# Summing a scan's output states: GpSimd adds halves of every other unit in the first chunk

## The chip, the cores and the metric

The kernel runs on one core of a Trainium2 chip. The metric is the device time of one execution in microseconds (us). TensorE is PE in the profile, VectorE is DVE, ScalarE is ACT, GpSimd is POOL, SyncE (which issues the DMAs here) is SP.

## The reference

The input is 64 series of 750 samples. Each is cut into 10 patches of 128 samples, hop 64, so there are 640 tokens. What is computed for them, all in float32:

```python
h = patches @ tok_W.T + tok_b                        # 512 wide
h = h + attn(layernorm(h))                           # attn: see below
h = h + swiglu(layernorm(h))                         # 512 -> 2048 -> 512
# attn(x): x + mamba(rmsnorm(x)), then + swiglu(rmsnorm(.))
# mamba(x):
z, xv, Bm, Cm, dt_in = split(x @ in_proj_w.T)
dt = softplus(dt_in @ dt_proj_w.T + dt_proj_b)       # 1024 channels
h[t] = exp(dt[t] * A) * h[t-1] + dt[t] * x[t] * B[t] # 16 states per channel
y[t] = sum over the 16 states of C[t] * h[t]
out = ((y + D_skip * x) * silu(z)) @ out_proj_w.T
```

The sum over 16 states in the line for y is what the change is about.

## The kernel before

The layout is features on the 128 partitions, tokens along the free axis. The tokens are worked in two chunks: c = 0 with 290 tokens (29 series of 10) and c = 1 with 350.

The recurrence is cut into **units**. The 1024 channels are KI = 8 tiles (m) of 128 channels; the 16 states of a channel are QU = 4 quarters (q) of NQ = 4 states. Unit u of a chunk is the pair (m, q), so there are 32 units in each chunk, 64 in all. For each unit:

- SP loads `bb` (rows of B spread over the partitions, line 359) and `cb` (rows of C, line 375) from DRAM, 580 KB each in chunk 0. `load_b(u)` is issued in the slot of unit u - 2. The rows of C of a tile m were stored before by `store_c` (line 363) from `c_rows`, which ScalarE copies from a PSUM bank at line 629.
- GpSimd makes the input term, `hs` = dtx * bb (`input_term`, line 443), for the four states at once, 128 x 1160 elements in chunk 0; at q = 0 it first makes `dtx` (line 433). `hs` has NH = 4 buffers.
- ScalarE makes the decay, exp(dt * A), in PSUM (`da`, line 538).
- VectorE scans (line 734), one state at a time, and multiplies by C, two states at a time (`times_c`, line 745), writing into `hs` again.
- The four states are summed. In chunk 0 TensorE does it (`state_sum`, line 949): four products with the identity matrix, accumulated over the tile's four units in the PSUM bank `work[SUM]`. Every float32 product shows as two records in the trace, so a unit has eight. In chunk 1 GpSimd adds (`add_states`, lines 456 to 469) into `acc`, and TensorE sums only two halves per tile (`ysum`).
- VectorE's `gate_y` (lines 758, 762) takes the finished sum of a tile, in the slot of the next tile's unit q = 1.

All engines go through the same list of **slots**, `schedule()`, one for each unit, with other work (**steps**) put into each: the projections `in_dt`, `in_x`, `in_b`, `in_c`, `in_z`, `dtp`, `xs` for later tiles, then for chunk 1 (`tokc`, `mean`, `ln1`, `rms1`), and in the slots of chunk 1 the MLP of chunk 0. The order on every engine is fixed by this list. ScalarE and VectorE take some steps one slot later than TensorE (`late(slots, 1)`), GpSimd and SP two slots later.

- TensorE, slot of unit u: part of the steps, then `state_sum(u - 2)`, then the other steps; when u % 4 is 1 the sum comes first. `xs`, `dtp`, `in_c` and `in_z` use a ring of three PSUM banks, so one waits until ScalarE has read the step three before it.
- GpSimd, slot of unit u: `input_term(u + 1)`, then `add_states(u - 1)` (which did nothing in chunk 0), then the steps: `softplus` (lines 475, 477, 479, the last one writes `dt`), which stands in the even slots that have a `dtp`. `input_term(u)` waits for its `bb` and for the state sum of unit u - 4, whose buffer it takes.
- ScalarE: decays for the next unit, and between them the steps. Its own part of the softplus (lines 655 to 662) waits for GpSimd's softplus of the tile before (`dt_ready`).

Of the kernel before, what the change touches and what calls it, by code (L numbers as in the profile page):

```python
# [29 lines left out]
KI = DI // P  # L30
HT = HID // P
NQ = 4
QU = NS // NQ
# [36 lines left out]
def unit_of(u):  # L70

    return u // UNITS, u % UNITS // QU, u % QU


def piece(u, p):
    c = u // UNITS
    return PIECE0[c] + u % UNITS * NP[c] + p


def products_through(u):  # L80

    return piece(u, NP[u // UNITS] - 1) // 2 + 1
# [60 lines left out]
def late(slots, lag, kinds=LATE):  # L143
    def lag_of(i, s):
        return lag if i == 1 or (s[0] in kinds and slots[i][0] is not None) else 0
    return [(unit, [s for j in range(max(0, i - lag), i + 1) for s in slots[j][1] if lag_of(j, s) == i - j])
            for i, (unit, _) in enumerate(slots)]
# [30 lines left out]
def build(nc, patches, tok_w, small, w_in, w_dt, w_stream, out):  # L178
# [10 lines left out]
    with ExitStack() as ctx:  # L189
# [3 lines left out]
        def sem(name):  # L193
            return ctx.enter_context(nc.semaphore(name))
# [70 lines left out]
        scan_done, c_times, th_done = sem("scan_done"), sem("c_times"), sem("th_done")  # L265
        added, h_summed, skip_done, y_done = sem("added"), sem("h_summed"), sem("skip_done"), sem("y_done")
# [12 lines left out]
        def full(eng, name):  # L279
            b, n = uses[last_name(name)]  # L280
            eng.wait_ge(bank_full[b], n + 1)
# [4 lines left out]
        def freed(eng, name):  # L286

            b, n = uses[name]
            eng.wait_ge(bank_free[b], n + 1)
# [4 lines left out]
        def h(c, k):  # L294
            return h_all[:, k, OFF[c]:OFF[c] + TS[c]]

        def a(c, k):
            return a_all[:, k, OFF[c]:OFF[c] + TS[c]]
# [20 lines left out]
        def on_dve(k):  # L319
            return k % DVE_SHARE == DVE_SHARE - 1  # L320
# [5 lines left out]
        def splits_at(s):  # L326
            if s == ("out", NCH - 1, KD - 2):
                return range(NW - 1)
            if is_split(s) and split_of[s] + NW - 1 < SPLITS:
                return [split_of[s] + NW - 1]  # L330
            return []

        def adds_through(u):

            return 7 * (u // QU - KI) + 2 * (u % QU) + 1

        block = ctx.enter_context(nc.Block())

# [79 lines left out]
        @block.gpsimd  # L418
        def _(pool):
            def split_low(k):  # L420
                pool.wait_ge(w_hi_done, k + 1)
                nc.gpsimd.tensor_tensor(ws[:, k % NW, 1, :], wraw[:, split_loads[k] % NRAW, :],  # L422
                                        ws[:, k % NW, 0, :].bitcast(F32), ALU.subtract).then_inc(w_lo_pool, 1)

            def input_term(u):
                c, m, q = unit_of(u)
                t, n = c * KI + m, TS[c]
                if q == 0:
                    pool.wait_ge(dt_ready, t + 1)
                    freed(pool, ("xs", c, m))  # L430
                    if t >= 2:
                        pool.wait_ge(dbx_done, QU * (t - 1))
                    nc.gpsimd.tensor_tensor(dtx[:, t % 2, 0:n], dt[:, m, 0:n], xf[:, m, 0:n],
                                            ALU.mult).then_inc(dtx_done, 1)
                    pool.wait_ge(dtx_done, t + 1)
                pool.wait_ge(bb_loaded[u % NB], 16 * (u // NB + 1))
                if u >= NH:
                    v = u - NH
                    if v < UNITS:
                        pool.wait_ge(h_summed, v + 1)  # L440
                    else:
                        pool.wait_ge(added, adds_through(v + 1 if v % QU == 0 else v))
                nc.gpsimd.tensor_tensor(hs[:, u % NH, 0:NQ * n].rearrange("p (n t) -> p n t", t=n),  # L443
                                        dtx[:, t % 2, 0:n].unsqueeze(1).to_broadcast([P, NQ, n]),
                                        bb[:, u % NB, 0:NQ * n].rearrange("p (n t) -> p n t", t=n),
                                        ALU.mult).then_inc(dbx_done, 1)

            def add_states(u):
                c, m, q = unit_of(u)
                if c == 0:  # L450
                    return
                w = 2 * TS[c]
                lo, hi = hs[:, u % NH, 0:w], hs[:, u % NH, w:2 * w]
                pool.wait_ge(c_times, products_through(u))
                if q <= 1:
                    nc.gpsimd.tensor_tensor(lo, lo, hi, ALU.add).then_inc(added, 1)
                if q == 0:
                    return
                n, total = adds_through(u), acc[:, 0:w]
                if q == 1:  # L460
                    if m >= 1:
                        full(pool, ("ysum", c, m - 1))
                    pool.wait_ge(added, n - 1)
                    nc.gpsimd.tensor_tensor(total, hs[:, (u - 1) % NH, 0:w], lo, ALU.add).then_inc(added, 1)
                else:
                    pool.wait_ge(added, n - 2)
                    nc.gpsimd.tensor_tensor(total, total, lo, ALU.add).then_inc(added, 1)  # L467
                    pool.wait_ge(added, n - 1)
                    nc.gpsimd.tensor_tensor(total, total, hi, ALU.add).then_inc(added, 1)

            def softplus(c, m):
                i, n = KI * c + m, TS[c]
                pool.wait_ge(sp_act, 3 * i + 3)

                nc.gpsimd.tensor_tensor(sp_u[:, 0:n], sp_w[:, 0:n], sp_u[:, 0:n], ALU.subtract).then_inc(sp_small, 1)
                pool.wait_ge(sp_small, 2 * i + 1)
                nc.gpsimd.tensor_tensor(sp_l[:, 0:n], sp_l[:, 0:n], sp_u[:, 0:n], ALU.subtract).then_inc(sp_small, 1)
                pool.wait_ge(sp_small, 2 * i + 2)
                nc.gpsimd.tensor_tensor(dt[:, m, 0:n], dt[:, m, 0:n], sp_l[:, 0:n], ALU.add).then_inc(dt_ready, 1)

            def residual(c, o):
                pool.wait_ge(res_done, KD * c + o + 1)
                nc.gpsimd.tensor_tensor(h(c, o), h(c, o), a(c, o), ALU.add).then_inc(hres_done, 1)

            for i, (unit, steps) in enumerate(late(slots, 2)):
                if unit == 0:
                    input_term(0)
                if unit is not None and unit + 1 < NCH * UNITS:
                    input_term(unit + 1)
                if unit is not None and unit >= 1:  # L490
                    add_states(unit - 1)
                if i == len(slots) - 1:
                    add_states(NCH * UNITS - 1)
                for s in steps:
                    if s[0] == "dtp":
                        softplus(s[1], s[2])
                    for k in splits_at(s):
                        if not on_dve(k):
                            split_low(k)
                    if s[0] == "out":  # L500
                        residual(s[1], s[2])

        @block.scalar
        def _(act):
# [51 lines left out]
            def gated_high(n):  # L556
                act.wait_ge(gated_raw, n + 1)
                gated_free(act, n)
                if n == 4 * HH * (NCH - 1):
                    act.wait_ge(added, adds_through(NCH * UNITS - 1))  # L560
                nc.scalar.copy(gated[:, 0, n % HH, 0:TS[NCH - 1]], gated_f[:, n % 2, 0:TS[NCH - 1]]).then_inc(gated_hi, 1)
# [364 lines left out]
        def _(pe):  # L926
# [15 lines left out]
            def state_sum(u):  # L942
                c, m, q = unit_of(u)
                n = TS[c]
                if q == 0 and m >= 1:
                    pe.wait_ge(y_done, m)
                pe.wait_ge(c_times, products_through(u))
                for i in range(NQ):
                    last = nc.tensor.matmul(work[SUM][:, 0:n], sm[:, S_IDENT:S_IDENT + P], hs[:, u % NH, i * n:(i + 1) * n],  # L949
                                            start=(q == 0 and i == 0), stop=(q == QU - 1 and i == NQ - 1))  # L950
                last.then_inc(h_summed, 1)

            def split_products(w, x, *ready):
# [169 lines left out]
```

## Time and profile before

| what | value |
|---|---|
| median of 3 runs | 705.84 us (lowest 703.69) |
| profiled execution | 703.4 us |
| its span, first to last instruction | 701.6 us |
| PE busy | 645.4 us, 92% |
| DVE busy | 427.3 us, 61% |
| POOL busy | 422.7 us, 60% |
| ACT busy | 340.9 us, 49% |
| chain that ended last | PE 62%, DVE 14%, DMA 10%, issue 5%, ACT 4%, POOL 4% |
| units of chunk 0 | about 34 to 213 us of the span |

Busy time is the union of an engine's instructions. The chain that ended last is followed back from the last instruction, at each step to what released it. PE records are pipelined, so the duration of a group in a timeline is from its first start to its last end. Times in timelines and windows count from the start of the span.

### The profile page before, as it was taken

What the parts mean: (1) busy time and instruction counts of PE and PEld (TensorE: products, weight loads), DVE (VectorE), ACT (ScalarE), POOL (GpSimd) and SP (SyncE); (2) the same over time, 40 slices, a digit from 0 to 9 for tenths busy, and PEclk for the clock granted to TensorE, in tenths of its full rate; (3) what the DMA queues carried; (4) which work ended last, traced back from release to release, by engine and by line L of the source; (5) the groups of instructions that cost most, each with busy time, mean ns of one, the idle gap of its engine ahead of it and who ended that gap; (6) DMA issues with size and microseconds to landing.
All of it is one profiled execution on the core that took longest, in us unless ns stands there. A gap on an engine that the chain in (4) does not pass through costs nothing.

```text
span 701.6 us, 8678 instructions
## 1 busy us (share of the span) xinstructions
PE 645.4 (92%) x2878; PEld 513.4 (73%) x2878; DVE 427.3 (61%) x660; ACT 340.9 (49%) x649; POOL 422.7 (60%) x236
## 2 busy tenths in 40 slices
PE   5969897799986989999979999999999999899998
PEld 3647674466554657777756777765799999799998
DVE  5097787898885878877986988871323132332132
ACT  4368889358886843323333323311444353543441
POOL 0276667445774999977784788743454655255551
PEclk9979999999999899999998999999999999999999
DMA  8788987499799797988784988842443444243521
GB/s 346 237 294 288 333 265 292 153 332 309 240 402 375 240 385 255 346 294 327 280 316 141 344 325 307 286 126 84 132 139 122 149 137 135 61 136 117 165 68 42
DMA packets 49164, 163.50 MB, mean 233 GB/s; under 512 B 4320, under 2 KB 18528, under 8 KB 48480
## 3 DMA queue, kind: packets, MB, share of 16 engines
q1 hardware_dynamic: 49120, 162.95, 66.7%
q8 instruction: 23, 0.38, 0.2%
q14 instruction: 21, 0.17, 0.1%
HBM read 145.24 MB, written 17.69 MB: 232 GB/s over the span
## 4 chain that ended last, share of the span: by engine, by line
PE 62%; DVE 14%; DMA 10%; issue 5%; ACT 4%; POOL 4%; SPq 0%; DVEq 0%; ACTq 0%; POOLq 0%
PE work L939 48%; PE da L939 13%; DMA bb<-b_rows 8%; DVE da L734 8%; DVE hs L745 3%; POOL hs L443 3%; ACT da L538 1%; PE work L949 1%; DMA b_rows<-sq 1%; DMA c_rows<-c_rows 1%; DMA sm<-small 0%; DVE work L758 0%; DVE a L796 0%; DVE gated_n L852 0%; DVE sq L813 0%
## 5 line engine op out<-in xcount | busy, mean ns | idle before, releaser
L734 DVE TENSOR_TENSOR_SCAN da<-da,hs 128x290 f32<-128x290 f32 (+1 forms) x256 | 198.3, 817 | 58.7 <-POOL hs L443 44.9
L443 POOL TENSOR_TENSOR hs<-dtx,bb 128x1160 f32<-128x1160 f32 (+1 forms) x64 | 171.0, 2676 | 79.0 <-DMA bb<-b_rows 40.1
L538 ACT ACTIVATE da<-dt,a_neg 128x261 f32<-128x261 f32 (+1 forms) x256 | 118.1, 494 | 134.1 <-DVE hs L745 133.9
L422 POOL TENSOR_TENSOR ws<-wraw,ws 128x1024 fp32r<-128x1024 f32 x40 | 101.4, 2536 | 92.8 <-ACT ws L546 92.8
L939 PE MATMUL work<-sq,wraw 128*128 128x290 f32 x512 | 126.5, 407 | 3.7 <-DVE sq L813 2.1
L939 PEld LDWEIGHTS work<-sq,wraw 128*128 128x128 f32 x512 | 96.4, 189 | 33.7 <-issue 5.1
L939 PE MATMUL work<-hn,win 128*128 128x290 f32 (+1 forms) x336 | 104.9, 462 | 16.1 <-DVE hn L804 8.0
L745 DVE TENSOR_TENSOR hs<-da,cb 128x580 f32<-128x580 f32 (+1 forms) x128 | 105.2, 822 | 7.1 <-DVE sq L829 0.2
L939 PEld LDWEIGHTS work<-hn,win 128*128 128x128 f32 x336 | 66.6, 202 | 50.5 <-issue 21.8
L546 ACT CAST ws<-wraw 128x1024 fp32r<-128x1024 f32 x48 | 50.3, 1048 | 70.9 <-PE work L939 36.0
L939 PE MATMUL work<-hn,ws 128*128 128x350 f32 x456 | 75.3, 323 | 1.6 <-DVE hn L900 1.6
L939 PEld LDWEIGHTS work<-hn,ws 128*128 128x128 f32 x456 | 73.4, 189 | 1.9 <-issue 1.9
L949 PE MATMUL work<-hs,sm 128*128 128x290 f32 x256 | 70.0, 417 | 0.0
L939 PE MATMUL work<-gated_n,wraw 128*128 128x290 f32 x256 | 64.1, 408 | 1.1 <-DVE gated_n L852 1.1
L949 PEld LDWEIGHTS work<-hs,sm 128*128 128x128 f32 x256 | 49.8, 195 | 17.6 <-issue 1.0
L939 PEld LDWEIGHTS work<-gated_n,wraw 128*128 128x128 f32 x256 | 48.3, 189 | 16.2 <-DVE gated_n L852 2.1
L939 PE MATMUL da<-hn,ws 128*128 128x350 f32 x312 | 51.7, 323 | 0.0
L939 PEld LDWEIGHTS da<-hn,ws 128*128 128x128 f32 x312 | 50.3, 189 | 0.0
L467 POOL TENSOR_TENSOR acc<-acc,hs 128x700 f32<-128x700 f32 x16 | 26.7, 1668 | 33.5 <-DVE hs L745 33.5
L846 DVE TENSOR_TENSOR pair<-th,work 128x350 f32<-128x350 f32 x20 | 10.4, 520 | 56.5 <-PE work L939 53.4
L939 PE MATMUL work<-gated,ws 128*128 128x350 f32 x240 | 39.3, 323 | 0.0
L939 PEld LDWEIGHTS work<-gated,ws 128*128 128x128 f32 x240 | 38.8, 188 | 0.0
(107 smaller groups left out, 669.1 us busy)
## 6 DMA issues: line engine op xcount, KB each, us to landing
wraw<-w_stream SPq DMA_DIRECT2D x104, 512.0 KB, 4.0
bb<-b_rows SPq DMA_DIRECT2D x32, 700.0 KB, 6.7
cb<-c_rows SPq DMA_DIRECT2D x32, 700.0 KB, 4.8
bb<-b_rows SPq DMA_DIRECT2D x32, 580.0 KB, 8.6
cb<-c_rows SPq DMA_DIRECT2D x32, 580.0 KB, 7.5
c_rows<-c_rows SPq DMA_DIRECT2D x8, 875.0 KB, 9.1
c_rows<-c_rows SPq DMA_DIRECT2D x8, 725.0 KB, 5.4
win<-w_in SPq DMA_DIRECT2D x4, 1024.0 KB, 13.0
```

What stands on the lines that cost most here:

```text
L422: nc.gpsimd.tensor_tensor(ws[:, k % NW, 1, :], wraw[:, split_loads[k] % NRAW, :], ws[:, k % NW, 0, :].bitcast(F32), ALU.subtract).then_inc ...
L443: nc.gpsimd.tensor_tensor(hs[:, u % NH, 0:NQ * n].rearrange("p (n t) -> p n t", t=n), dtx[:, t % 2, 0:n].unsqueeze(1).to_broadcast([P, NQ, ...
L467: nc.gpsimd.tensor_tensor(total, total, lo, ALU.add).then_inc(added, 1)
L538: last = nc.scalar.activation(dst, src, ACT.Exp, scale=a_neg[:, j:j + 1])
L546: nc.scalar.copy(ws[:, k % NW, 0, :], wraw[:, i % NRAW, :]).then_inc(w_hi_done, 1)
L734: nc.vector.tensor_tensor_scan(da[:, k % ND, 0:w], da[:, k % ND, 0:w], hs[:, u % NH, p * w:(p + 1) * w], 0.0, ALU.mult, ALU.add).then_inc( ...
L745: nc.vector.tensor_tensor(hs[:, u % NH, here].rearrange("p (i w) -> p i w", w=w), da[:, k % ND:k % ND + 2, 0:w], cb[:, u % NC, here].rearr ...
L846: nc.vector.tensor_tensor(gated_f[:, i % 2, 0:n], th[:, i % 2, 0:n], bank((s, "up")), ALU.mult).then_inc(gated_raw, 1)
L939: last = nc.tensor.matmul(dst, w, x, start=(k == 0), stop=(k == len(pairs) - 1))
L949: last = nc.tensor.matmul(work[SUM][:, 0:n], sm[:, S_IDENT:S_IDENT + P], hs[:, u % NH, i * n:(i + 1) * n], start=(q == 0 and i == 0), stop ...
```

## The change

In chunk 0, for units with odd q, `add_states` on GpSimd now waits for the unit's products and adds the second half of `hs` (states 3 and 4 of the unit, 580 columns) onto the first, in place. TensorE's `state_sum` for these units waits for that add instead of for the products, and sums two blocks of 290 columns instead of four. Units with even q are as they were. `adds_through`, which counts GpSimd's adds for the semaphore `added`, gets the 16 new adds.

```diff
         def adds_through(u):
 
-            return 7 * (u // QU - KI) + 2 * (u % QU) + 1
+            c, m, q = unit_of(u)
+            return 2 * (u // QU) + (q + 1) // 2 if c == 0 else 2 * KI + 7 * (u // QU - KI) + 2 * q + 1
...
             def add_states(u):
                 c, m, q = unit_of(u)
-                if c == 0:
+                if c == 0 and q % 2 == 0:
                     return
                 w = 2 * TS[c]
                 lo, hi = hs[:, u % NH, 0:w], hs[:, u % NH, w:2 * w]
                 pool.wait_ge(c_times, products_through(u))
-                if q <= 1:
+                if c == 0 or q <= 1:
                     nc.gpsimd.tensor_tensor(lo, lo, hi, ALU.add).then_inc(added, 1)
-                if q == 0:
+                if c == 0 or q == 0:
                     return
...
-                pe.wait_ge(c_times, products_through(u))
-                for i in range(NQ):
+
+                k = NQ - 2 * (q % 2)
+                if q % 2 == 1:
+                    pe.wait_ge(added, adds_through(u))
+                else:
+                    pe.wait_ge(c_times, products_through(u))
+                for i in range(k):
                     last = nc.tensor.matmul(work[SUM][:, 0:n], sm[:, S_IDENT:S_IDENT + P], hs[:, u % NH, i * n:(i + 1) * n],
-                                            start=(q == 0 and i == 0), stop=(q == QU - 1 and i == NQ - 1))
+                                            start=(q == 0 and i == 0), stop=(q == QU - 1 and i == k - 1))
                 last.then_inc(h_summed, 1)
```

## Rows read from the trace of the kernel before

**Rows 1.** The page, busy time, share of the span and instructions of each engine.

```profile
PE 645.4 (92%) x2878; PEld 513.4 (73%) x2878; DVE 427.3 (61%) x660; ACT 340.9 (49%) x649; POOL 422.7 (60%) x236
```

**Rows 2.** Who waited for whom, 34 to 232 us: total, times, longest.

```profile
DVE da L734 <- POOL hs L443: 44.1, 13, 18.9
POOL hs L443 <- DMA bb<-b_rows: 36.8, 14, 5.7
```

**Rows 3.** The chain that ended last, one cycle: start us, us, what.

```profile
81.59 2.45 POOL hs L443
...
92.72 0.34 ACT c_rows L629
...
93.49 9.89 DMA bb<-b_rows
```

**Rows 4.** GpSimd's timeline: start us, us, instruction, idle time before and its releaser.

```profile
83.99 0.80 POOL L475 TENSOR_TENSOR pair<-sp_w,pair 128x290 f32<-128x290 f32 x1
...
86.30 4.84 POOL L443 TENSOR_TENSOR hs<-dtx,bb 128x1160 f32<-128x1160 f32 x2
...
97.42 2.45 POOL L443 TENSOR_TENSOR hs<-dtx,bb 128x1160 f32<-128x1160 f32 x1 [3.11 <-issue]
...
144.51 2.43 POOL L443 TENSOR_TENSOR hs<-dtx,bb 128x1160 f32<-128x1160 f32 x1 [10.42 <-PE work L949]
```

**Rows 5.** ScalarE's timeline, softplus steps and one copy of c_rows.

```profile
64.43 0.51 ACT L655 ACTIVATE pair<-work,sm 128x290 f32<-128x290 f32 x1 [1.61 <-POOL dt L479]
...
86.39 0.49 ACT L655 ACTIVATE pair<-work,sm 128x290 f32<-128x290 f32 x1
...
89.70 0.39 ACT L629 COPY c_rows<-work 128x290 f32<-128x290 f32 x1
...
178.39 0.55 ACT L655 ACTIVATE pair<-work,sm 128x350 f32<-128x350 f32 x1 [0.71 <-issue]
...
228.98 0.55 ACT L655 ACTIVATE pair<-work,sm 128x350 f32<-128x350 f32 x1 [0.60 <-issue]
```

**Rows 6.** Windows: length, busy time of each engine, granted clock, DMA share, GB/s.

```profile
59.60:81.50 21.90, 21.41 (x85) 15.34 (x85) 17.03 (x25) 17.24 (x37) 14.85 (x11) 1.00 0.86 286
...
88.75:90.20 1.45, 0.86 (x4) 0.34 (x2) 1.36 (x4) 1.45 (x5) 1.45 (x1) 1.00 0.00 0
...
180.20:182.50 2.30, 1.86 (x7) 0.88 (x5) 1.39 (x4) 2.27 (x7) 2.30 (x2) 1.00 0.00 0
183.40:231.00 47.60, 40.26 (x134) 25.46 (x133) 34.54 (x48) 37.02 (x70) 29.17 (x21) 0.94 1.00 362
```

**Rows 7.** GpSimd's groups by shape: count, busy us, mean ns, idle before.

```profile
L443 POOL TENSOR_TENSOR hs<-dtx,bb 128x1160 f32<-128x1160 f32 x32 | 77.9, 2442 | 64.3 <-DMA bb<-b_rows 32.8 <-PE work L949 20.6 <-issue 10.7
...
L467 POOL TENSOR_TENSOR acc<-acc,hs 128x700 f32<-128x700 f32 x16 | 26.7, 1668 | 33.5 <-DVE hs L745 33.5
...
L433 POOL TENSOR_TENSOR dtx<-dt,xf 128x290 f32<-128x290 f32 x8 | 6.4, 800 | 0.7 <-ACT xf L639 0.7
```

**Rows 8.** TensorE's timeline around the sums of units 7 and 31.

```profile
81.96 2.12 PE L949 MATMUL work<-hs,sm 128*128 128x290 f32 x8
...
87.41 2.19 PE L939 MATMUL work<-hn,win 128*128 128x290 f32 x8 [2.30 <-ACT dt L656]
...
226.24 1.50 PE L939 MATMUL work<-sq,sm 32*128 32x350 f32 x2 [4.98 <-ACT z L645]
227.67 4.24 PE L949 MATMUL work<-hs,sm 128*128 128x290 f32 x8
```

**Rows 9.** The chain again: the sum of unit 13, and 263 us.

```profile
120.69 1.96 PE work L949 x8
...
263.12 63.19 PE work L939 x256
```

**Rows 10.** VectorE's timeline, a scan of unit 36.

```profile
246.22 1.67 DVE L734 TENSOR_TENSOR_SCAN da<-da,hs 128x350 f32<-128x350 f32 x2 [0.82 <-POOL hs L443]
```

**Rows 11.** Windows, a stretch at the half clock.

```profile
225.60:232.30 6.70, 6.06 (x12) 3.71 (x13) 5.31 (x7) 5.99 (x13) 6.54 (x6) 0.50 0.62 256
```

## The prediction

> **What bounds the kernel now.** I began with the page's sums: TensorE is busy 92% of the span and GpSimd 60%, which would make any work taken off TensorE look welcome [rows 1]. But shares are means over stages, so I next read who waits for whom between 34 and 232 us, the stretch in which the change lives. There the long waits are not TensorE's: VectorE's scans wait 44 us for GpSimd's input terms, and these wait 37 us for the loads of `bb` [rows 2]. The chain in order of time shows a loop. The `bb` of unit 9 has landed, GpSimd multiplies at 81.59, VectorE scans, ScalarE copies `c_rows` at 92.72, SP then issues the next `bb`, and that takes 9.89 us to land at 103.4 [rows 3]. That is 21.9 us for four units, most of it DMA. The windows tell where this loop has air: between 88.75 and 90.20, and again between 180.20 and 182.50, the DMA engines move nothing, though they are busy before and after; from 183.40 to 231.00 they are busy all the time [rows 6]. So in the steady part the DMA engines work off a queue, run dry, and wait until ScalarE's copy of `c_rows` (89.70) lets SP store it and issue the next loads [rows 5]. What makes ScalarE late makes the next four units late.
>
> What makes it late? ScalarE's timeline says it: its softplus step at line 655 waits for GpSimd's `dt` at 64.43 (1.61 us idle, released by POOL dt L479) and again at 178.39 after 0.71 us. At 86.39 it shows no wait, but there GpSimd's last softplus instruction ended at 86.30, where its next product starts [rows 4, 5]. So the chain of waits names VectorE and the DMA, and GpSimd's softplus ends at the same moment: a hidden twin of the path with about 0.1 us of slack. TensorE in the same cycle has `in_c` done long before it is copied, and idles before 87.41 for ScalarE [rows 8].
>
> **The change, part by part.** *TensorE* loses two of four products in 16 of 32 units. One unit's eight records take 1.96 us on the chain at the full clock [rows 9], so 0.98 us goes each time, 15.7 us in all. Most of that is not on the path: TensorE waits for ScalarE in every cycle [rows 8]. It counts in one place, 116 to 125 us, where the chain runs through TensorE (first steps of the second chunk) and holds the sums of units 12 and 13; unit 13's halves: -0.98 us [rows 9].
>
> *GpSimd* gains 16 adds with an output of 128x580. No such form is in the trace. Bounds: 700 elements take 1.67 us, 290 take 0.80 us, 1160 (a product that also reads two inputs) take 2.44 us [rows 7]. By proportion, 580 elements give 1.38 us; the line through 290 and 700 gives 0.80 + 290 x 2.12 ns = 1.41 us, the one through 290 and 1160 gives 0.80 + 290 x 1.89 ns = 1.35 us. I take 1.38, since the same adds of the second chunk are its nearest kin; 16 x 1.38 = 22 us of GpSimd work.
>
> Against the slower engine the Trainium skill (GPSIMD Engine Reference, Engine selection) says that an elementwise add belongs on VectorE, GpSimd being about twice as slow with two inputs. No row shows VectorE adding this form; it would not alter the sum, which uses GpSimd's own rows.
>
> *Where the adds stand.* GpSimd adds unit u right behind the input term of u + 2 and ahead of the softplus of that slot. Behind it are queued that softplus, then the input term of u + 3; ScalarE's softplus waits for the first and VectorE's scan for the second. Its wait for the products is free in the steady part: VectorE is done with unit 7 and waits for unit 9's input term [rows 2], and the add of unit 7 would start at 84.0, when that term ends. GpSimd was idle before that term, but the add stands behind it, so the idle time can't be used. There are six kinds of places:
> - Units 3, 7, 11 and 23 (softplus taken by ScalarE at 64.43, at 86.39, a cycle later, and at 178.39 [rows 5]): the full 1.38 us goes into ScalarE, then into the `c_rows` copy or the `z` behind it, and the DMA engines (or TensorE, after unit 11) stay idle that much longer. 4 x 1.38 = +5.5 us. Two of the four are seen in the waits, one is argued from the 0.1 us of slack, one is its repetition a cycle later.
> - Units 1, 5, 9, 13, 25, 29: GpSimd idles after the softplus (3.11 us before 97.42 [rows 4]); the adds are hidden there. With that cover gone they would cost 1.38 each, 8 us.
> - Units 15, 17, 19: no softplus in these slots, and VectorE is the busy engine; unit 17's add makes GpSimd wait for VectorE, but GpSimd had 10.42 us of idle time there, until TensorE's sum let it go on at 144.51 [rows 4]. 0.
> - Unit 21: its softplus delays ScalarE by 1.3 us, ScalarE has about that much air before unit 25. +0.1.
> - Unit 27: delays ScalarE too, but the DMA queue is never empty from 183.40 to 231.00, as the weight preload stands in it [rows 6]; loads issued later land when the queue allows. 0; if the queue were not full, +1.4.
> - Unit 31: on TensorE eight records take 4.24 us at the half clock [rows 8, 11], four would take 2.1. But its add pushes the softplus, for which ScalarE waits at 228.98 [rows 5], and with it the bank that TensorE's next product needs. VectorE's scan at 246.22 waits for GpSimd too, which sets the pace there [rows 10]. Between -0.9 and +1.4; I take +0.5.
>
> *TensorE's new wait.* The sum of unit 7 began at 81.96; now it begins at about 85.4, when the add is done, and ends at 86.5. Behind it are queued `xs` and the next `in_c`, and this waited for ScalarE until 87.41 anyway [rows 8]. VectorE's gate reads the sum behind unit 9's scans, later still. So the wait is under cover by 0.9 us, and by 2.3 with ScalarE late as well.
>
> **Sum.** +5.5 - 1.0 + 0.1 + 0.5 = +5.1 us. From 263 us on the chain is mostly TensorE products that the change doesn't touch, 63 us of them in one piece at the start [rows 9], so a shift at its start is a shift of the end. Against the profiled execution (703.4 us, span 701.6) that gives 708.5; against the median of 705.84, 710.9. The shown runs are 703.69 and 705.84, so I take the middle, 709.7.
>
> **Rivals.**
> 1. *The clock.* Waits lengthen TensorE's idle stretches: before the sum of unit 7 by some 3.4 us. In the trace an idle stretch of 4.98 us before 226.24 went with the half clock from 225.60 to 232.30 (1.2 instead of 2.4 GHz), one of 2.3 us before 87.41 did not [rows 8, 11]. At the half clock a full state sum costs 4.24 instead of 2.12 us. If every late add brought on a stretch of 6.7 us, and the products in it lay on the path, each of the four cycles would lose up to 3.4 us more: 13.6 + 5.1 = +18.7, 724 us, slower by over 2%. It decides only when `in_c` and what follows end after ScalarE's turn to copy them, some 3 us later than now (87.41 + 2.19 against 92.72) [rows 3, 8]; the half clock adds about 2 us to one projection. So it should stay mostly covered, except near 120 us, where it could cost 1 to 3 us. The Trainium skill (TensorE: Matmul & The Clock Gate, Why this matters for your kernels) warns of idle gaps between bursts for this reason; the trace agrees at 226 us.
> 2. *TensorE is the bound after all.* If TensorE's queue held back ScalarE in each cycle, the 15.7 us would come back: up to 690 us. Against it: TensorE waits for ScalarE's banks in every cycle, and the DMA idles because of ScalarE. A part, 3 to 5 us, is thinkable between 110 and 160 us, where it is the busier engine.
> 3. *No change.* The add before a softplus is covered, because GpSimd was not what held ScalarE, or the DMA queue catches up in the air it has (it is busy 86% of a cycle [rows 6]). For it: the chain does not name GpSimd's softplus in two of the four cycles. Time: within 2 us of before, 703 to 706.
>
> **Numbers.** Forecast, +2 to +9 us: 0.55. Clock, +9 to +20: 0.2. No change: 0.16. Gain: 0.09. The range from 703 to 718 leaves out the larger gains and the worst of the clock, about 2 in 10. Two per cent, about what a measurement of this kernel can tell from no change, is 14 us: only the outer half of the clock rival reaches it on one side and the outer third of the gain on the other. Faster 0.03, within 0.89, slower 0.08.
>
> **What would show it.** In the changed trace: adds of about 1.38 us directly after an input term; ScalarE's line 655 idle some 1.3 us for POOL dt L479 in the cycles of units 7 and 11, where it did not wait before; the DMA engines' idle stretches longer by 1.4 us; a cycle from one `bb` landing to the fourth next of 23.3 instead of 21.9 us; TensorE idle before the sums of odd units. The prediction is wrong if the cycles keep their length (rival 3), if the half clock is seen in more stretches and the chain runs through TensorE's L939 between 60 and 230 us (rival 1), or if chunk two starts earlier than now (rival 2).

## The result, and the profile after

The changed kernel takes 709.70 us (median of 5 runs, 707.81 to 711.56) against 705.47 before: ratio 1.0066, 95% interval 1.0039 to 1.0093, so 4.7 us slower (2.8 to 6.6). By the 2% bound that is no change; it is clear of the noise all the same. The 705.47 is the median of five runs too, one of which took 1611.85 us and is left out of the ratio; the other four lie between 703.69 and 705.84.

On the page of the changed kernel TensorE is busy 0.7 us less than before and GpSimd 21.7 us more [rows 1]:

```profile
PE 644.7 (91%) x2814; PEld 507.9 (72%) x2814; DVE 428.2 (60%) x660; ACT 341.5 (48%) x649; POOL 444.4 (63%) x252
```

64 records are gone from TensorE (16 units, two products of two records each), and yet its busy time is almost the same, as more of the rest ran at the half clock (below). GpSimd's groups of the changed kernel by shape, mean ns of one:

```profile
L444 POOL TENSOR_TENSOR hs<-dtx,bb 128x1160 f32<-128x1160 f32 x32 | 77.9, 2442 | 45.1 <-DMA bb<-b_rows 29.7 <-PE work L955 10.5 <-issue 4.8
...
L457 POOL TENSOR_TENSOR hs<-hs 128x580 f32<-128x580 f32 x16 | 22.6, 1414 | 5.2 <-DVE hs L746 5.2
```

An add takes 1.41 us, and the input terms beside it take 2442 ns as before [rows 7]. Now the chain of the changed kernel, the same cycle as in [rows 3] (start us, us):

```profile
82.42 2.44 POOL hs L444
84.85 1.36 POOL hs L457
86.22 0.77 POOL pair L476
...
88.56 0.50 ACT pair L656
...
94.90 0.34 ACT c_rows L630
95.26 0.37 SPq L364
95.67 9.80 DMA bb<-b_rows
105.55 2.43 POOL hs L444
```

The add (L457) and GpSimd's softplus are on the chain, where VectorE's scans were. (The timeline of GpSimd gives the add as 84.80 and 1.41 us; the chain counts it from the end of the product.) From one product of GpSimd to the fourth next it is 105.55 - 82.42 = 23.13 us; before it was 103.45 - 81.59 = 21.86. ScalarE's timeline of the changed kernel, the softplus steps that answer to [rows 5] (idle before, releaser):

```profile
65.39 0.51 ACT L656 ACTIVATE pair<-work,sm 128x290 f32<-128x290 f32 x1 [2.03 <-POOL dt L480]
...
88.56 0.50 ACT L656 ACTIVATE pair<-work,sm 128x290 f32<-128x290 f32 x1 [0.83 <-POOL dt L480]
...
111.69 0.50 ACT L656 ACTIVATE pair<-work,sm 128x290 f32<-128x290 f32 x1 [1.17 <-POOL dt L480]
...
181.64 0.55 ACT L656 ACTIVATE pair<-work,sm 128x350 f32<-128x350 f32 x1 [1.91 <-issue]
...
205.98 0.55 ACT L656 ACTIVATE pair<-work,sm 128x350 f32<-128x350 f32 x1 [2.16 <-issue]
```

Against before, the starts are late by 0.96, 2.17, 3.39, 3.25 and 4.83 us (64.43, 86.39, 108.30, 178.39 and 201.15 before). At 88.56 and 111.69 ScalarE waits where it did not. At 181.64 the view names no releaser ("issue"), as it named none at 178.39 before; GpSimd's last softplus instruction ended at 178.31 before and ends at 181.55 now, 0.1 us ahead of ScalarE both times. The windows of the changed kernel (length, busy times, granted clock, DMA share, GB/s):

```profile
65.90:70.00 4.10, 3.58 (x9) 2.62 (x10) 2.53 (x6) 4.04 (x11) 4.10 (x2) 0.63 0.00 0
...
112.40:116.30 3.90, 3.57 (x8) 2.57 (x9) 2.35 (x6) 3.84 (x11) 3.90 (x2) 0.50 0.00 0
...
181.80:186.60 4.80, 3.99 (x8) 2.42 (x8) 2.43 (x6) 4.74 (x12) 4.80 (x3) 0.52 0.00 0
186.70:234.50 47.80, 39.79 (x122) 23.83 (x120) 34.74 (x49) 36.07 (x68) 33.47 (x25) 0.89 0.99 361
```

The DMA engines stand still for 4.8 us before 186.6, where the stretch was 3.7 us in the kernel before (from 179.7), and they are then busy all the time, as in [rows 6]. The first two windows belong to the cycles of units 3 and 11. The same two places in the kernel before:

```profile
66.30:69.00 2.70, 2.21 (x10) 1.45 (x9) 2.55 (x5) 2.70 (x8) 2.70 (x2) 1.00 0.00 0
...
110.30:112.90 2.60, 2.60 (x7) 1.87 (x6) 2.35 (x6) 2.60 (x8) 2.60 (x2) 0.50 0.00 0
```

All three idle stretches have grown, by 1.1 to 1.4 us. TensorE in the changed kernel, sums of units 7 and 31 (compare [rows 8]):

```profile
86.27 1.25 PE L955 MATMUL work<-hs,sm 128*128 128x290 f32 x4 [3.36 <-POOL hs L457]
...
89.60 4.20 PE L940 MATMUL work<-hn,win 128*128 128x290 f32 x8 [0.82 <-ACT dt L657]
...
230.80 2.30 PE L955 MATMUL work<-hs,sm 128*128 128x290 f32 x4 [1.02 <-POOL hs L457]
234.64 8.80 PE L940 MATMUL work<-hn,win 128*128 128x350 f32 x24 [1.54 <-ACT dt L657]
...
267.30 8.03 PE L940 MATMUL work<-sq,wraw 128*128 128x290 f32 x25 [2.06 <-DVE sq L814]
```

The long TensorE run of chunk 0's MLP starts at 267.30, 4.18 us later than at 263.12 before [rows 9].

The profiled execution is the slowest of the five, 711.56 us, 8.2 more than the profiled one before. What lies behind 263 us is the clock. First two windows of the changed kernel, then one of the kernel before:

```profile
268.40:271.70 3.30, 3.30 (x8) 2.29 (x7) 1.71 (x3) 1.19 (x1) 3.30 (x3) 0.50 0.32 124
374.20:384.30 10.10, 8.42 (x19) 5.40 (x18) 3.27 (x7) 3.59 (x6) 2.45 (x1) 0.50 0.26 91
```

```profile
365.50:372.20 6.70, 4.20 (x8) 2.52 (x8) 2.06 (x4) 3.23 (x6) 5.19 (x3) 0.50 0.79 287
```

3.3 us of products at the half clock, which before ran at the full one, cost 1.65 us; 8.42 instead of 4.20 us at the half clock cost 2.1. 4.18 + 1.65 + 2.1 = 7.9 of the 8.2. The other four runs lie 1.3 to 3.8 us lower, at mean granted clocks of 0.954 to 0.959 where the profiled one has 0.952, so not every run has lost all of this. That none of it is due to the change is not shown.

### The profile page after: what moved, and what is told of

Read it like the earlier page. It is cut to its first block, busy times and chain, and to the rows that moved or that the text cites. A ratio compares the mean times of both kernels' runs of the same rounds, so it can differ in the third digit from the quotient of the medians.

```text
span 709.8 us, 8566 instructions
## 1 busy us (share of the span) xinstructions
PE 644.7 (91%) x2814; PEld 507.9 (72%) x2814; DVE 428.2 (60%) x660; ACT 341.5 (48%) x649; POOL 444.4 (63%) x252
## 4 chain that ended last, share of the span: by engine, by line
PE 59%; DVE 11%; DMA 11%; POOL 8%; ACT 5%; issue 4%; SPq 0%; DVEq 0%; ACTq 0%; POOLq 0%
PE work L940 46%; PE da L940 13%; DMA bb<-b_rows 9%; DVE da L735 6%; POOL hs L444 4%; DVE hs L746 3%; ACT da L539 2%; POOL hs L457 2%; PE work L955 1%; DMA b_rows<-sq 1%; DMA c_rows<-c_rows 1%; DMA sm<-small 1%; POOL pair L476 1%; POOL pair L478 1%; ACT pair L656 0%
## 5 line engine op out<-in xcount | busy, mean ns | idle before, releaser
L940 PE MATMUL work<-sq,wraw 128*128 128x290 f32 x512 | 131.2, 418 | 3.7 <-DVE sq L814 2.1
L940 PE MATMUL work<-hn,win 128*128 128x290 f32 (+1 forms) x336 | 111.7, 485 | 17.8 <-DVE hn L805 8.2
L940 PEld LDWEIGHTS work<-sq,wraw 128*128 128x128 f32 x512 | 99.5, 195 | 35.3 <-issue 5.1
L940 PEld LDWEIGHTS work<-hn,win 128*128 128x128 f32 x336 | 69.5, 212 | 57.0 <-issue 26.5
L955 PE MATMUL work<-hs,sm 128*128 128x290 f32 x192 | 55.1, 424 | 12.3 <-POOL hs L457 12.3
L457 POOL TENSOR_TENSOR hs<-hs 128x580 f32<-128x580 f32 (+1 forms) x32 | 49.3, 1541 | 18.2 <-DVE hs L746 18.1
L955 PEld LDWEIGHTS work<-hs,sm 128*128 128x128 f32 x192 | 36.8, 195 | 27.5 <-POOL hs L457 15.7
```

Source lines behind the costliest of these rows:

```text
L940: last = nc.tensor.matmul(dst, w, x, start=(k == 0), stop=(k == len(pairs) - 1))
```

## The experiments

"Step" below is the time by which the end of VectorE's second product of a unit is later than in the profile before, taken behind the place less the same ahead of it; the add of unit v shows from the products of unit v + 3 on. All differences in us are the ratio times 705.

**The adds ahead of the input term** (in GpSimd's slot, first chunk only):

```diff
+                if unit is not None and 1 <= unit <= UNITS:
+                    add_states(unit - 1)
                 if unit is not None and unit + 1 < NCH * UNITS:
                     input_term(unit + 1)
-                if unit is not None and unit >= 1:
+                if unit is not None and unit > UNITS:
                     add_states(unit - 1)
```

> The changed kernel with each first-chunk add moved ahead of the input term of its slot, into the time in which GpSimd waits for bb; same adds, same sums. Theory (place): the 1.2 to 1.4 us in front of ScalarE's softplus in the cycles of units 3, 7, 11 and 23 go, and what is left is TensorE's relief: 1 to 2 us faster than before the change, 703.5 to 705 against 705.5. Rival A (load: 22 us more on GpSimd cost wherever they stand): still +4 to +5, about 710. Rival B (TensorE's wait and its half clock cost the time): the sums are released earlier too, so a gain like the theory's; this run doesn't tell B from it.

Measured: 703.29 us, ratio 0.9979 (0.9963 to 0.9995), -1.5 us. GpSimd's timeline in this kernel, and ScalarE's softplus:

```profile
79.09 1.41 POOL L457 TENSOR_TENSOR hs<-hs 128x580 f32<-128x580 f32 x1
82.86 2.43 POOL L444 TENSOR_TENSOR hs<-dtx,bb 128x1160 f32<-128x1160 f32 x1 [2.37 <-DMA bb<-b_rows]
85.25 0.80 POOL L476 TENSOR_TENSOR pair<-sp_w,pair 128x290 f32<-128x290 f32 x1
```

```profile
87.64 0.50 ACT L658 ACTIVATE pair<-work,sm 128x290 f32<-128x290 f32 x1
```

The same 1.41 us now stand in GpSimd's wait for `bb`, of which 2.37 us are left, and ScalarE takes its softplus without idle time. With the same work and the same number of adds the kernel takes 6.2 us less than with the change. Rival A (load) has fallen; B is not touched.

**The adds behind the softplus** of the slot:

```diff
                 for s in steps:
                     ...
+                if unit is not None and 1 <= unit <= UNITS:
+                    add_states(unit - 1)
```

> The changed kernel with each first-chunk add moved behind the softplus of its slot. Theory (place): ScalarE's softplus is as early as before; the next input term ends some 1.4 us later and VectorE's scan some 0.7 us, which the DMA queue hides, so -1 to +1.5 us, 704.5 to 707. Rival B (TensorE's wait): the sums of odd units come 2.3 us later still than in the changed kernel, so at least its +4.7, rather +7, 710 to 713. Rival A (load): +4 to +5.

Measured: 707.70 us, 1.0044 (1.0021 to 1.0067), +3.1 us: more than I expected and less than B. In its profile VectorE's unit 9 is 0.6 us earlier than before and unit 13 0.2 us later, so the cycles are as expected. The loss comes at unit 15, a step of 2.6 us. TensorE's timeline there:

```profile
116.72 2.70 PE L942 MATMUL work<-pat,tokw 128*128 128x350 f32 x4 [2.39 <-ACT z L648]
119.21 3.76 PE L957 MATMUL work<-hs,sm 128*128 128x290 f32 x8
```

The four records ahead of it take 2.70 instead of 1.74 us and the sum of unit 12 takes 3.76 instead of 2.12: a half-clock stretch lies on the one part of the chain that runs through TensorE, the mechanism of the forecast's first rival in one place. A further 1.3 us is lost behind unit 23's add, and there TensorE is on the chain as well:

```profile
181.49 2.30 PE L957 MATMUL work<-hs,sm 128*128 128x290 f32 x4 [5.21 <-POOL hs L457]
...
185.19 5.04 PE L942 MATMUL work<-hn,win 128*128 128x350 f32 x8
```

```profile
115.70:122.50 6.80, 5.79 (x11) 3.82 (x12) 2.47 (x4) 6.62 (x13) 1.92 (x2) 0.50 1.01 370
...
180.50:190.60 10.10, 9.11 (x16) 4.87 (x16) 7.71 (x12) 6.05 (x15) 9.84 (x8) 0.50 0.58 193
```

TensorE waits 5.21 us for the add, the projection behind it takes 5.04 us at the half clock where it took 2.62, and ScalarE's copy of `c_rows` follows. So rival B's mechanism is real where the adds come last in the slot. That all timed runs lose the time in this way is not shown.

**The load alone**: the add writes to `acc`, which nothing reads then, and TensorE sums all four blocks. GpSimd also gets waits on its own earlier adds, which the lines below leave out:

```diff
-                    nc.gpsimd.tensor_tensor(lo, lo, hi, ALU.add).then_inc(added, 1)
+                    nc.gpsimd.tensor_tensor(acc[:, 0:w], lo, hi, ALU.add).then_inc(added, 1)
...
-                k = NQ - 2 * (q % 2)
-                if q % 2 == 1:
-                    pe.wait_ge(added, adds_through(u))
-                else:
-                    pe.wait_ge(c_times, products_through(u))
+                k = NQ
+                pe.wait_ge(c_times, products_through(u))
```

> The adds stand where the change put them, but write into another buffer that nothing reads; TensorE sums all four blocks and waits only for the products, as before the change. Theory (place): the whole cost without the relief, 4 x 1.38 + 0.1 + 0.5 to 1.4 = +6 to +7, 711.5 to 712.5. Rival B (TensorE's wait): 0, 705.5. Rival A (load): +5 to +6.

Measured: 709.82 us, 1.0057 (1.0035 to 1.0079), +4.0 us. Rival B (TensorE's wait) expected nothing here and has fallen: without any new wait of TensorE the cost is there. ScalarE, and the DMA engines, in this kernel:

```profile
65.33 0.50 ACT L662 ACTIVATE pair<-work,sm 128x290 f32<-128x290 f32 x1 [2.04 <-POOL dt L486]
```

```profile
65.80:69.90 4.10, 2.91 (x11) 2.07 (x12) 2.57 (x5) 4.04 (x12) 4.10 (x2) 1.00 0.00 0
```

The steps at units 6, 10, 14 and 26 are 1.37, 1.20, 1.31 and 1.35 us, 5.2 in all. Unit 19 is a step of 1.3 as well, and it is not an add's (see the four units below). The timed cost is below the 6 to 7 us that I gave; where the difference goes is open, and the interval reaches 5.6.

**The relief alone**: TensorE sums two blocks, no add, so that half of the states of the odd units are left out of y:

```diff
-                for i in range(NQ):
+                k = NQ - 2 * (q % 2)
+                for i in range(k):
```

> The kernel before, with TensorE summing only the first two blocks of units with odd q in the first chunk: half of the states of these units are left out of y. No add and no new wait. Theory: TensorE's relief is worth 1.0 us at unit 13 and up to 0.9 at unit 31, -1 to -2, 703.5 to 704.5. Rival C (TensorE bounds the first chunk): a large part of its 15.7 us, -5 to -15.

Measured: 703.76 us, 0.9977 (0.9959 to 0.9996), -1.6 us. Rival C has fallen: taking the 15.7 us of products (their time at the full clock) off TensorE is worth 1.6. Not all of it became idle time, since TensorE is busy 640.5 us in this profile, only 4.9 less than before. TensorE's projection at the place of [rows 8], and the window around it:

```profile
87.71 4.20 PE L939 MATMUL work<-hn,win 128*128 128x290 f32 x8 [2.25 <-ACT dt L656]
```

```profile
85.30:92.00 6.70, 4.45 (x10) 3.14 (x10) 6.21 (x11) 6.11 (x15) 6.62 (x5) 0.50 0.48 183
```

It takes 4.20 us at the half clock, as in the changed kernel, and yet no add is waited for here. The clocks of the timed runs also part the clock from the cost. The relief alone, granted 0.954 to 0.961 (the change: 0.952 to 0.959), gains 1.6 us; the load alone, granted 0.961 to 0.971 (the kernel before: 0.966 to 0.973), costs 4.0. So a lower clock by itself is not what makes the change slower; whether the relief would be worth more at the clock of the kernel before is open.

**The four units alone, and the twelve others** (units 3, 7, 11, 23 in the first; `adds_through` counts accordingly):

```diff
-                if c == 0 and q % 2 == 0:
+                if c == 0 and u not in ADDED_UNITS:
...
-                k = NQ - 2 * (q % 2)
-                if q % 2 == 1:
+                k = NQ - 2 * (u in ADDED_UNITS)
+                if u in ADDED_UNITS:
```

> The change for units 3, 7, 11 and 23 alone, the four whose add was held to be on the path; the other twelve odd units are summed by TensorE as before. Theory (place): 4 x 1.38 = +5.5 and no relief at unit 13, 710 to 711.5. Rivals A and B (load, or TensorE's waits, each spread over the 16 adds): a quarter of 4.7, +1 to +1.5, about 706.8.

> The change for the twelve other odd units (1, 5, 9, 13, 15, 17, 19, 21, 25, 27, 29, 31). Theory (place): -1.0 at unit 13, +0.1 at 21, 0 to +1.4 at 31, so -1 to +0.5, 704.5 to 706. Rivals A and B: three quarters of 4.7, +3.5, about 709.

Measured: the four 711.67 us, 1.0093 (1.0069 to 1.0117), +6.6 us; the twelve 702.95 us, 0.9978 (0.9958 to 0.9999), -1.6 us. This is the plainest answer: a quarter of the adds costs as much as all of them or more (4.9 to 8.2 us against 2.8 to 6.6), and the other three quarters cost nothing or gain a little. Together they make +5.0, the change's 4.7. GpSimd and ScalarE in the kernel with the four:

```profile
62.20 1.41 POOL L458 TENSOR_TENSOR hs<-hs 128x580 f32<-128x580 f32 x1
63.57 0.80 POOL L477 TENSOR_TENSOR pair<-sp_w,pair 128x290 f32<-128x290 f32 x1
```

```profile
65.96 0.50 ACT L657 ACTIVATE pair<-work,sm 128x290 f32<-128x290 f32 x1 [1.36 <-POOL dt L481]
```

Its steps are 1.37, 1.36, 1.31 and 1.36 us, 5.4 together. There is one more, 1.3 us at unit 19, where no add is near. TensorE is on the chain there; its row in this kernel, then in the kernel before:

```profile
137.62 10.31 PE L941 MATMUL work<-hn,win 128*128 128x350 f32 x24 [4.49 <-DVE hn L806]
```

```profile
133.41 8.98 PE L939 MATMUL work<-hn,win 128*128 128x350 f32 x24 [4.49 <-DVE hn L804]
```

The same 24 records take 1.33 us longer, at a granted clock of 0.50 from 136.9 to 143.6; before, only half as long a stretch was at 0.50. The kernels with the load alone, with the adds of 8 columns, with the adds ahead and with the swap below have a step of 1.1 to 1.3 us there too and half-clock stretches of 6.8 us, the change has neither. In the kernel with the twelve, unit 30 is a step of 1.35 late (the add of unit 27), and unit 32 has it back: the DMA queue hid it, as forecast. The add of unit 31 then costs a step of 1.4. Its profiled execution takes as long as the one before (703.36 and 703.4), so where the twelve gain the 1.6 us is seen only in part: 0.98 us at unit 16, from unit 13's two products.

**The waits without the length**: adds of 8 columns, 0.20 us each. Of the second halves only 8 columns get into y.

```diff
+                if c == 0:
+                    lo, hi = lo[:, 0:8], hi[:, 0:8]
```

> The change with adds of 8 columns of each half instead of 580, at the same place, and TensorE waits for them and sums two blocks: of the second half only 8 columns get into y, the rest is left out. It keeps every wait of the change and takes nearly all of the adds' length away. Theory (place): a tiny add may last 0.1 to 0.3 us; 4 x 0.2 - 1.0 - 0.5 = about -1, 704 to 705.5. Rival B (the wait behind the input term costs the time): +3 to +5, 709. Rival A (load): near the theory's.

Measured: 703.82 us, 0.9985 (0.9964 to 1.0006), -1.1 us. TensorE waits for an add behind the input term as in the change, and it costs nothing that can be told from the relief alone.

**The bound itself**: `in_c` ahead of `dtp` in the kernel before, on all engines.

```diff
-    return [[("dtp", c, m), ("in_c", c, m)], [("xs", c, m), ("in_c", c, m + 1)],
+    return [[("in_c", c, m), ("dtp", c, m)], [("xs", c, m), ("in_c", c, m + 1)],
```

> The kernel before, with the steps in_c and dtp swapped in their slot on all engines, so that ScalarE copies c_rows before its softplus and not behind it. If ScalarE's copy is what leaves the DMA engines idle 1.5 to 2.5 us in a cycle (the loop on which the prediction rests), this takes the idle time away in five cycles: -4 to -8 us, 697 to 702. If VectorE or GpSimd would set the same pace anyway: 0 to -2.

Measured: 696.56 us, 0.9886 (0.9862 to 0.9910), -8.0 us. ScalarE's timeline, and windows: the times at which the DMA engines were idle before, and the longest stretch in which they are idle now:

```profile
83.28 0.39 ACT L629 COPY c_rows<-work 128x290 f32<-128x290 f32 x1
...
84.38 0.48 ACT L655 ACTIVATE pair<-work,sm 128x290 f32<-128x290 f32 x1
```

```profile
66.75:68.20 1.45, 1.45 (x7) 1.13 (x6) 1.35 (x3) 0.72 (x3) 1.45 (x2) 1.00 1.06 349
88.75:90.20 1.45, 0.82 (x4) 0.42 (x3) 1.42 (x3) 0.86 (x3) 1.45 (x2) 1.00 0.95 360
...
103.85:108.20 4.35, 3.59 (x9) 2.56 (x10) 3.96 (x8) 4.29 (x12) 3.86 (x4) 0.64 0.00 0
...
180.20:182.50 2.30, 2.30 (x10) 1.34 (x8) 2.27 (x4) 1.44 (x5) 2.14 (x4) 1.00 0.98 345
```

The copy that stood at 89.70 is made at 83.28, and at the times of [rows 6] the DMA engines are busy. As this kernel runs up to 6 us ahead there, equal times are not equal places; counted over 50 to 235 us, the idle stretches of over 0.5 us sum to 16.2 us where they were 19.7. That of the first cycle is gone, those of the second and of the one at 180 us are down to 1.2 and 1.4 us, and that of the third, at 110 us before, has grown from 2.7 to 4.4. The mean granted clock of its runs, 0.966 to 0.978, is that of the kernel before. So ScalarE's turn for `c_rows` did set the pace of most of the first chunk.

**The change on top of that**, and the adds ahead of the input terms on top of it (both edits as above):

> The change as it is, with in_c and dtp swapped in their slot as in the run before (which took 8.7 us off the kernel before, 696.6). ScalarE's first copy of c_rows now stands ahead of its softplus, so an add that delays the softplus no longer delays that store and leaves no idle time of the DMA engines. Theory (place): the change costs at most 0 to +2.5 us on top of the swap, 696.5 to 699. If the cost had nothing to do with that copy: the same +4.7 on top of it, 701.

> The swap of in_c and dtp together with the adds ahead of the input terms. Theory: the two gains add up nearly, -8.7 - 1.5, 695 (693.5 to 697). If the swap already took the time that the relief gave: 696.6.

Measured, beside a median of 706.72 before: 700.23 us, 0.9896 (0.9862 to 0.9930), and 699.29 us, 0.9890 (0.9857 to 0.9923). On top of the swap the change costs 0.10%, 0.7 us, instead of 4.7; the intervals allow some 3 more, and the two profiled executions are 2.6 us apart (697.57 and 695.00). The 0.7 is a difference of two ratios to different medians of the kernel before (705.25 and 706.72) and can hardly be told from 2.6. Between the two profiles VectorE is 2.5 us later by unit 8 and no later from there to unit 15, where without the swap two more steps of 1.2 us came. By unit 25 it is 0.3 us later and by unit 35, behind unit 31's add, 3.4. So the cost is smaller with the swap and lies elsewhere; how much is left is open. The adds ahead of the input terms show no further gain there, against what I expected.

## Why the prediction was right

- *The bound.* The hidden twin of the chain, GpSimd's softplus with 0.1 us of slack, was there: it is on the chain after, and moving ScalarE's copy ahead of it gave 8.0 us. "Most of it DMA" was a misreading: the load is the longest piece of the cycle, but 9.89 of 21.86 us.
- *The add.* 1.41 us measured, 1.38 taken.
- *4 x 1.38 = 5.5.* From the landing of unit 5's `bb`, 0.43 us early, to the softplus that starts 0.96 late: 1.39. Then 1.21 (2.17 - 0.96) and 1.22 (3.39 - 2.17), and at unit 23, from 1.89 late at unit 25's products to 3.25, 1.36. Sum 5.2. The second and third are less than the add because ScalarE had 0.1 us of slack and because the loads ahead took 0.1 us less (9.85 and 9.80 us, 9.97 and 9.89 before).
- *Unit 13's relief, -1.0.* The chain after has it, four records instead of eight:

```profile
121.55 1.96 PE work L955 x8
123.51 0.59 PE work L940 x2
124.10 0.98 PE work L955 x4
```

  VectorE's unit 16 has the 0.98 us back, here, in the relief alone and with the twelve units; with the load alone and with the four units, where unit 13 is summed in full, it has not.

- *Unit 27, 0.* ScalarE is 4.83 us late, unit 32's last product 2.7 late: the DMA queue took it back, and with it 0.75 us of what the units ahead had cost, which the forecast did not have.
- *Unit 31, +0.5.* Units 32 and 33 are 2.7 and 3.3 late, the MLP's start 4.18: between 0.9 and 1.5, at the upper end of the bounds and 0.4 to 1.0 above the term. At the half clock the sum is shorter by 1.9 us, but TensorE waits 1.02 us for the add ahead of it and 1.54 us for ScalarE's bank behind it.
- *Unit 21, +0.1.* No loss is seen between unit 22 (2.15 late) and unit 25 (1.89).
- *Covered places.* The twelve units as a whole gain 1.6 us (0.1 to 3.0).
- *Sum.* +5.1 forecast; 4.2 up to the MLP's start in the profile, 4.7 by the ratio. Unit 31 was too low and unit 27 too high by about the same, which is luck. So is the hit of the median to the last digit (709.7 and 709.70): it came from taking the middle of two bases that are 2.4 us apart. And the forecast's 2% as the least that can be told is too coarse: the interval is 0.27% to either side.
- *Rival 1, the clock.* TensorE's wait before unit 7's sum was forecast as 3.4 us and is 3.36. The half clock did come more often:

```profile
87.50:94.20 6.70, 5.88 (x13) 3.74 (x13) 5.40 (x9) 5.17 (x14) 6.62 (x5) 0.50 0.27 96
111.40:118.10 6.70, 5.37 (x11) 3.73 (x12) 5.11 (x9) 5.69 (x15) 6.70 (x5) 0.50 0.30 98
```

  `in_c` at 89.60 takes 4.20 us there and ends at 93.8, ahead of ScalarE's copy at 94.9: covered, with 1.1 us left. The Trainium skill's warning about gaps (TensorE: Matmul & The Clock Gate, Why this matters for your kernels) came true for the clock, not for the time. But that the new waits brought the half clock, as the rival had it, is not shown: the relief alone has the same 4.20 us behind idle stretches of 1.91 and 2.25 us and without any new wait. With the adds behind the softplus such a stretch did get onto the chain.
- *Rival 2 and 3* are refuted by the relief alone (1.6 us) and by the four units (6.6 us).

## What to carry to other kernels

An engine's idle time is only worth something at the place in its queue where the new work stands: the same 16 adds cost 4.7 us behind the wait for a load and gained 1.5 us ahead of it. Look for what ends within a tenth of a microsecond of the chain that the profile names; here that twin, GpSimd's softplus, carried the cost. And before giving an engine less to do, ask who waits for it: 15.7 us off TensorE were worth 1.6, while the order of two steps was worth 8.

## What was not expected of the hardware

Less work for TensorE did not make it as much less busy. 15.7 us of products (at the full clock) were taken away, and its busy time fell by 0.7 us in the changed kernel, by 4.9 with the relief alone and by 9.9 with the adds ahead of the input terms, as more of what was left ran at the half clock (1.2 GHz). The new waits are not needed for that: the mean granted clock is 0.952 to 0.959 over the runs of the change, 0.954 to 0.961 with the relief alone and 0.966 to 0.973 over the runs of the kernel before that were taken beside the latter.

Equal kernels also get different clocks from run to run, and their time goes with it: the twelve runs with the adds behind the softplus spread from 703.11 us at 0.963 to 711.47 us at 0.952. Half-clock stretches behind 263 us make up some 4 of the 8.2 us between the two profiled executions.
